# First attention: the second application's products on the other partition half, and VectorE moving them back

## What is computed

```
qkv = x @ Wqkv + bqkv                                # 8 heads of 64
scores = einsum("bhnd,bhmd->bhnm", q, k) * SCALE
top_val = top_k(scores, 64)[0][..., -1:]             # 65 keys: all but the lowest stay
attn = softmax(where(scores < top_val, -inf, scores))
v_curr = v; res = 0
for i in range(3):                                   # three applications of the same attn
    v_curr = attn @ v_curr
    res = res + gelu(alphas_raw[i]) * v_curr
out = res @ Wout + bout
```

## Time and profile before

| | |
|---|---|
| median of three runs | 1669.5 us |
| the profiled execution | 1673.58 us |
| its span, first to last instruction | 1671.8 us |
| busy over the span: TensorE, VectorE, ScalarE, GpSimd | 95%, 74%, 55%, 47% |
| granted TensorE clock, mean over the span | 0.979 |
| span of the first attention, from its first project_v to its last project_out | about 289 to 790 us |
| matmul rows / VectorE instructions of the span | 24380 / 3629 |

### The profile page before, as it was taken

How to read it: one execution, slowest core, us unless ns; L and a number is a source line. 1 busy time by engine, 2 the same in 40 slices (tenths; PEclk the granted TensorE clock), 3 DMA queues, 4 the chain that set the end, 5 groups by cost and what they waited for, 6 DMA issues and landing times. The chain is left out here.

```text
span 1671.8 us, 62551 instructions
## 1 busy us (share of the span) xinstructions
PE 1589.5 (95%) x24380; PEld 1169.5 (70%) x24380; DVE 1242.6 (74%) x3629; ACT 912.6 (55%) x2409; POOL 784.4 (47%) x932
## 2 busy tenths in 40 slices
PE   7999999899999999997999998999999999879997
PEld 3333334677777777776567746888888888669997
DVE  2799926888888888885767764577777777778875
ACT  0111315666666666663544455666666666557753
POOL 0000000788888888885011102345555555645554
PEclk9999999999999999999989999999999999979998
DMA  9999940000000000000300000000000000135431
GB/s 338 355 373 355 350 160 1 3 4 4 3 4 4 4 4 4 3 4 10 106 1 1 1 1 6 3 9 21 25 18 25 18 25 18 37 114 152 137 85 41
DMA packets 73078, 118.06 MB, mean 71 GB/s; under 512 B 11627, under 2 KB 30366, under 8 KB 72828
## 3 DMA queue, kind: packets, MB, share of 16 engines
q1 hardware_dynamic: 65054, 100.04, 18.2%
q0 software_dynamic: 6096, 12.94, 2.2%
q10 hardware_dynamic: 1678, 1.43, 0.3%
HBM read 97.59 MB, written 18.61 MB: 70 GB/s over the span
## 5 line engine op out<-in xcount | busy, mean ns | idle before, releaser
L1700 PE MATMUL ps<-xn,s_a_wqkv 128*128 128x260 f32 x1024 | 277.4, 403 | 6.1 <-DMA s_a_wqkv<-in_f_b 3.0
L1700 PEld LDWEIGHTS ps<-xn,s_a_wqkv 128*128 128x128 f32 x1024 | 178.0, 192 | 52.0 <-issue 18.4
L1037 POOL TENSOR_TENSOR prob_a<-e_a,inv_sum_a 128x512 f32<-128x512 f32 x64 | 67.1, 1048 | 194.8 <-issue 113.4
L1566 DVE TENSOR_REDUCE neg_max_a<-ps 128x8 f32<-128x520 f32 x128 | 89.2, 697 | 73.3 <-PE ps L1674 50.2
L2323 POOL DMA_INDIRECT out<-h,xn x93 | 97.8, 1051 | 88.3 <-DVE h L2438 86.8
L1784 PE MATMUL ps<-s_a_wqkv,xn_pair_a 128*64 128x256 f32 x1024 | 138.9, 391 | 0.0
L1092 ACT ACTIVATE resT_a<-ps 128x260 f32<-128x260 f32 x256 | 85.2, 386 | 97.2 <-PE ps L1751 61.0
L1021 POOL TENSOR_TENSOR kept_a<-e_a,keep_a 128x585 f32<-128x585 f32 x64 | 87.2, 1362 | 70.4 <-issue 60.3
L921 POOL MEMSET cls_queries_a<- 128x1040 f32 x2 | 1.9, 966 | 250.9 <-POOLq L430 250.9
L1751 PE MATMUL ps<-probT_a,horner_a 64*64 64x65 f32 x2048 | 113.2, 228 | 2.0 <-DVE horner_a L1312 1.5
L1741 PE MATMUL ps<-dv_a,probT_a 64*64 64x64 f32 x2048 | 107.1, 223 | 3.0 <-DVE probT_a L1325 2.3
(11 more groups left out here) (305 smaller groups left out, 4663.6 us busy)
## 6 DMA issues: line engine op xcount, KB each, us to landing
x_chunk<-in_x_main SPq DMA_DIRECT2D x144, 512.0 KB, 11.0
xn<-pair_rows SPq DMA_DIRECT2D x93, 130.0 KB, 2.1
pair_rows<-pad_rows_m SPq DMA_DIRECT2D x29, 130.0 KB
s_f_all<-in_f_w SPq DMA_DIRECT2D x2, 1024.0 KB
x_ends<-in_x_tail SPq DMA_DIRECT2D x16, 96.0 KB, 5.6
out<-h,xn POOLq DMA_INDIRECT x93
s_w_tok<-in_w_tok SPq DMA_DIRECT2D x6, 192.0 KB, 8.9
pair_rows<-rows_m,slot_i_m POOLq DMA_INDIRECT x65, 2.5
```

The lines of the kernel that those rows point to most:

```text
L1566: last = nc.vector.tensor_reduce(neg_max[:, :, 0:CH], score(), AX.X, ALU.min)
L1700: nc.tensor.matmul(ps[:, QK_BANK[i], 0:QUAD], w_qkv[:, c * P:(c + 1) * P], xn[:, t.h * QUAD:(t.h + 1) * QUAD], start=True, stop=True).then ...
```

## The change

The second application goes to the crossed quarters. Its bank 3 then holds each head's result on the other head's partitions, and VectorE's add of a0 v, one instruction over 128 partitions before, becomes two instructions over 64 partitions, each reading PSUM from the one half and writing SBUF on the other. The third application and the class column go to the crossed quarters for the first image and to the own quarters for the second. So `project_out` needs the exchanged weights for the first image and the plain ones for the second: instead of 4 matmuls of 260 columns a quad it has 8 of 130, in two runs of 65. The order of issue inside a c is new as well.

```diff
--- before.py
+++ after.py
@@ -1309,8 +1309,14 @@
                 upto(dve, va_done, 2 * (t.s - lag) + 1 + n, 2 * pairs)
                 if n == 0:
                     upto(dve, dsum_done, t.s - 5, pairs)
-                nc.vector.tensor_tensor(flat(dc[n][:, (t.j - lag) % 2]), ps[:, 2 + n, :],
-                                        flat(va[n][:, (t.j - lag) % (2 + 2 * n)]), ALU.add).then_inc(c_done[n], 1)
+                out, add = flat(dc[n][:, (t.j - lag) % 2]), flat(va[n][:, (t.j - lag) % (2 + 2 * n)])
+                if n == 0:
+                    nc.vector.tensor_tensor(out, ps[:, 2, :], add, ALU.add).then_inc(c_done[0], 1)
+                else:
+                    for b in range(2):
+                        rows, other = slice(b * DH, (b + 1) * DH), slice((1 - b) * DH, (2 - b) * DH)
+                        last = nc.vector.tensor_tensor(out[rows], ps[other, 3, :], add[rows], ALU.add)
+                    last.then_inc(c_done[1], 1)
 
             def probs_out(t):
 
@@ -1737,8 +1743,9 @@
                     values = dv[:, k] if n == 0 else dc[0][:, (t.j - lag) % 2]
                     col = (i * CH + c) * DH
                     for b in range(2):
-                        rows = slice(b * DH, (b + 1) * DH)
-                        last = nc.tensor.matmul(ps[rows, 2 + n, col:col + DH], pt[rows, k, c, i, 1:SEQ],
+                        rows, half = slice(b * DH, (b + 1) * DH), b ^ n
+                        last = nc.tensor.matmul(ps[half * DH:(half + 1) * DH, 2 + n, col:col + DH],
+                                                pt[rows, k, c, i, 1:SEQ],
                                                 values[rows, i, c, :], start=True, stop=True)
                     if i == 1 and c == CH - 1:
                         last.then_inc(p_ps[n], 1)
@@ -1747,8 +1754,8 @@
 
                     k = (t.j - 6) % 4
                     for b in range(2):
-                        rows, other = slice(b * DH, (b + 1) * DH), slice((1 - b) * DH, (2 - b) * DH)
-                        last = nc.tensor.matmul(ps[other, R_BANK[i], c * SEQ:c * SEQ + cols],
+                        rows, half = slice(b * DH, (b + 1) * DH), b ^ (1 - i)
+                        last = nc.tensor.matmul(ps[half * DH:(half + 1) * DH, R_BANK[i], c * SEQ:c * SEQ + cols],
                                                 values[rows, (t.j - 6) % 2, i, c, :], pt[rows, k, c, i, 0:cols],
                                                 start=first, stop=not first)
                     if i == 1 and c == CH - 1 and not first:
@@ -1758,13 +1765,12 @@
                     for i in range(2):
                         if t.has(4):
                             order(0, i, c)
-                        if t.has(6):
-                            crossed(dc[1], i, c, SEQ, True)
-                    for i in range(2):
                         if t.has(5):
                             order(1, i, c)
-                        if t.has(6):
-                            crossed(dsum, i, c, 1, False)
+                    for values, cols, first in ((dc[1], SEQ, True), (dsum, 1, False)):
+                        for i in range(2):
+                            if t.has(6):
+                                crossed(values, i, c, cols, first)
 
             def project_v(t):
                 if not t.has(2):
@@ -1843,10 +1849,11 @@
                 sl = (t.j // 2) % 2
                 half = QUAD // 2
                 if masked:
-                    for c in range(CH):
-                        last = nc.tensor.matmul(ps[:, O_BANK, O_COL:O_COL + QUAD], w_out_sw[:, c, :],
-                                                res_t[:, sl, c].rearrange("p n i t -> p (n i t)"),
-                                                start=(c == 0), stop=(c == CH - 1))
+                    by_image = ps[:, O_BANK, O_COL:O_COL + QUAD].rearrange("p (n i t) -> p n i t", n=2, i=2)
+                    for i, w in enumerate((w_out_sw, w_out)):
+                        for c in range(CH):
+                            last = nc.tensor.matmul(by_image[:, :, i, :], w[:, c, :], res_t[:, sl, c, :, i, :],
+                                                    start=(c == 0 and i == 0), stop=(c == CH - 1 and i == 1))
                 for i, w in enumerate((w_out, w_out_sw) if not masked else ()):
                     for c in range(CH):
                         last = nc.tensor.matmul(ps[:, O_BANK, O_COL + i * half:O_COL + (i + 1) * half], w[:, c, :],
```

## The result

The changed kernel takes 1674.72 us in the median of 20 runs (1671.30 to 1682.46), the kernel before 1670.99 us in 20 runs beside them (1666.54 to 1679.15). The ratio is 1.0024, with a 95% interval of 1.0014 to 1.0035: 4.0 us more (2.3 to 5.8). That is a real loss, and for the most part under the 0.3% that the prediction counted as no change. The profiled execution of the changed kernel took 1673.38 us (span 1671.6), that of before 1673.58, the slowest of its first three. So the two profiles don't show the loss as a difference of spans; they show how each stage has changed.

A forecast was written before the change was run, and what follows sets the result against it. TensorE was taken to set the pace (busy 294.2 of 300 us), VectorE next with 43.1 us to spare. Terms 0 + 1 + 1 + 2 = +4 us on the median of 1669.5 gave 1673.5 us, range 1663 to 1684.

The forecast's parts named there:

- TensorE's two terms: TensorE's matmuls: 0 us for the second and third applications' products and +1 us for project_out.
- VectorE's two: VectorE's longer adds: +1 us where waits don't cover them in the middle, +2 us at the stage's start and end.
- The products, 0: TensorE's product steps: rows per quarter set the time, eight before and after, so a c stays 0.47 us, gain 0.
- project_out, +1: Output projection in 16 rows of 130 columns: -0.07 to +0.03 us a quad, -2 to +1 us in all, taken as +1.
- VectorE, +0.95 us a pair: Second order_out in two halves: three late starts, the sum 2.15 us after order 0 instead of 1.20.
- Covered, +1 in the middle: Middle of the attention: VectorE's waits just absorb the extra 0.95 us a pair; +1 us where they don't.
- Start and end, +2: Ends of the attention stage, where TensorE waits for VectorE: the 0.7 to 0.95 us paid in part, +2 us.
- Rival 1: TensorE's products: columns count, up to 0.47 us a pair shorter until VectorE bounds; 1664.5 us, chance 0.11.
- Rival 2: Second order_out: slower halves make VectorE the bound at 1.2 us extra a pair; 1686.5 us (1680 at 1.1), chance 0.24.
- Rival 3: New issue order inside a c: matmuls starting strictly in program order cost 0.08 us a pair; 1678.5 us, chance 0.12.

The follow-up runs named there:

- e2: The changed kernel with one add over all 128 partitions instead of two halves (values wrong): 1668.84 us against 1671.99 us, ratio 0.9982 to the kernel before.
- e3: The kernel before with its second order_out split into two 64-partition adds, each on its own partitions: 1678.53 us, ratio 1.0046 to the kernel before.
- e11: The kernel before with its second order_out split into two own-half adds everywhere but in the last steps (from step 64 on): ratio 0.9998.
- e10: The kernel before with its second order_out split into two own-half adds only in the last steps (from step 64 on): ratio 1.0014.
- e4: The changed kernel with one 128-partition add and without the class column's matmuls (output wrong): ratio 0.9831 to the kernel before.
- e5: The kernel before without the class column's matmuls (output lacks a term): ratio 0.9892 to the kernel before.
- e6: The changed kernel with one extra 256-element VectorE memset a pair, ahead of order 0: ratio 1.0054 to the kernel before.

## Why the prediction was right, point by point

The predicted time, 1673.5 us, is +4 us on the median of before, and the measured ratio is +4.0 us. As far as the runs place the time, the mechanism held: no gain on TensorE from columns, VectorE's longer adds mostly covered in the middle, a price at the end. The exact hit is luck. TensorE's two terms, predicted at 0 + 1, came to -3.0 us together (e2), and VectorE's two, predicted at 1 + 2, to about +7 us (e3, and the changed kernel against e2). Two errors of about 4 us cancelled.

- **The products, 0.** The mechanism held: a c takes 0.47 us, as the count of rows a quarter said, and the order of rows in other quarters doesn't matter. The size was a little off. Between the first row of the products and what follows them it is now 566.54 - 564.57 = 1.97 us, 2.01 before. A likely reason, not tested by itself: in the last c every quarter now ends with a one-column row, where the own quarters used to end with one of 64. That is 0.04 us a pair, 2.6 us in 64, in line with the shortest cycle (14.83 to 14.77, project_out's 0.03 us included) and e2 (-3.0 us). The prediction counted the rows, with 50 ns and 58 ns beside each other, and then used their mean alone.
- **project_out, +1.** 562.92 - 561.04 = 1.88 us against 1.85 in the earlier trace rows: 0.03 us a quad, as the upper bound had it. That the moving operand is two runs of 65 columns costs nothing visible.
- **VectorE, +0.95 us a pair.** The sum starts 2.13 us (559.54 to 561.67) and 2.14 us after order 0 in two neighbouring steps, 2.15 were predicted. Three starts are late, at 0.71, 0.70 and 0.72 us. What came to probs_out is less, since the wait for GpSimd took its share: in the means of 400 to 700 us it starts 3.03 us after order 0 instead of 2.62, so 0.41 us a pair; 0.64 was predicted.
- **Covered, +1 in the middle.** Nothing contradicts it, but it isn't settled to the microsecond: e11 is at 0.9998 (-3.2 to 2.5 us), and the changed kernel's middle took 392.13 us. Yet e3 minus e10 leaves some 5 us that are not in the last steps. The waits vanished as expected, and VectorE's busy time reached 288.84 us, 96% of the 300 (the prediction said 97% in one place and 285 us in another).
- **Start and end, +2.** The place was right, the working had a piece missing. From the first project_v (289.44 us before, 289.51 after) to the one at 353.98 and 353.83 us it took no longer than before, so the start paid nothing that shows. At the end I counted the wait alone, "paid in part", from 1.47 us upward; it became 2.33 us. What I left out is TensorE's clock: stretches at the lower level follow these pauses, and the matmuls in them take up to nearly twice as long. The rows behind the prediction had no such case, but the trace of before had a project_out of 3.58 us at its end, which was there to be read. The term is 2.3 us by timing (e10, -0.2 to 4.7), 3.0 us between the profiles of before and after, and 5 us between the two groups of profiles.
- **Rival 1** (columns count) fell with the c at 0.47 us and with e4 and e5. **Rival 2** (VectorE the bound) did not come about at 0.93 us a pair. Its price was too high as well: e6 has the 1.20 us a pair that it spoke of (0.93 and 0.27), and came to 1.0054, 9 us over before, not 17. **Rival 3** (strict order) fell: at the places where products of the same quarters now follow each other no shift appeared, a c still takes 0.47 us and the products as a whole got 0.04 us shorter. The rule of the Trainium skill that it rested on ("TensorE: Matmul & The Clock Gate", part 3) is not borne out for matmuls in different quarters.

## What to carry to other kernels

For small matmuls that share the array in quarters, count rows per quarter, the fullest quarter, and not columns; moving work between quarters gains only where the fullest one gets fewer rows. Splitting a VectorE add by partitions halves nothing and adds a late start at each change of the first partition, also for the next instruction that reads PSUM. Idle time of an engine behind the bound covers such work in a steady stretch, but not where the pipeline drains: there a pause of TensorE can cost more than itself, since the clock may fall behind it. When two versions differ by a few microseconds, put the granted clock of each stretch beside its length before looking for another cause.

## What was not expected of the hardware

- A late start isn't avoided by the order of the halves: it moved from the sum to probs_out (0.12 to 0.24 us behind the reciprocal), and order 0 to probs_out stayed at 3.03 us.
- A pause longer by 0.70 us was followed by a granted clock of 0.50 instead of 1.00, and by 3.56 instead of 2.02 us for the same project_out. But nearly the same waits at the end gave clocks of 0.88, 1.00 and 0.94 in three kernels.
- TensorE's pauses in the middle, 0.33 us a cycle of 15.16, vanished in e5, where an eighth of its rows was left out though no c became shorter (a cycle 14.65 us, busy 300.00 of 300). They lie multiples of 256 of TensorE's instructions apart (to within one) in every kernel that has them, which points to the supply of its program, written out in full and not looped; no run shows more.
